# Gathers and scatters that alternate in an expert loop, and an expert's w1 copied by SyncE's DMAs

## The reference

```python
x = x + tanh(g_xattn) * xattn(layernorm(x), ctx)            # q, k from ctx (128 features), softmax, mix
h = layernorm(x)
wgt, idx = top_k(softmax(gelu(h @ rw1) @ rw2), 2)           # 8 experts, 2 for each token
for e in range(8):
    Ye = gelu(h @ w1[e] + b1[e]) @ w2[e] + b2[e]            # w1[e] 256 x 1024, w2[e] 1024 x 256
    Ce = gelu(b1[e]) @ w2[e] + b2[e]
    for k in range(2):
        mask = idx[..., k] == e
        out += any(mask) * wgt[..., k] * where(mask, Ye, Ce)
return x + tanh(g_ffn) * out
```

## Time and profile before

| what | value |
|---|---|
| time, median of 3 runs | 244.16 us (242.99, 244.16, 244.80) |
| span of the profiled execution, first to last instruction | 240.2 us |
| PE, matmul busy | 174.1 us, 72% |
| VectorE busy | 178.3 us, 74% |
| ACT busy | 96.2 us, 40% |
| GpSimd busy | 118.0 us, 49% |
| expert loop, from the first half of pair 2 to that of pair 9 | 124.64 to 213.26 us |
| mean granted TensorE clock | 0.876 |

### The profile page before, as it was taken

How to read it: one execution, slowest core, us unless ns; L and a number is a source line. 1 busy time by engine, 2 the same in 40 slices (tenths; PEclk the granted TensorE clock), 3 DMA queues, 4 the chain that set the end, 5 groups by cost and what they waited for, 6 DMA issues and landing times.

```text
span 240.2 us, 5593 instructions
## 1 busy us (share of the span) xinstructions
PE 174.1 (72%) x1708; PEld 141.8 (59%) x1709; DVE 178.3 (74%) x352; ACT 96.2 (40%) x230; POOL 118.0 (49%) x144
## 2 busy tenths in 40 slices
PE   7876638818500176729997989989797979799691
PEld 2455426317400133629887979889797979687370
DVE  1399998999999899596956776767675767656264
ACT  1369527656585700603333342423333334233000
POOL 0033365991789209992337282746455464632100
PEclk9997988976855557779999999999999999999955
DMA  7893564785887504101001111110102020100096
GB/s 190 280 381 118 175 213 145 249 282 193 271 302 256 189 3 130 45 1 46 20 21 46 44 44 32 32 55 15 57 22 66 20 66 22 46 15 27 31 289 233
DMA packets 20625, 28.05 MB, mean 117 GB/s; under 512 B 2341, under 2 KB 17407, under 8 KB 20610
## 3 DMA queue, kind: packets, MB, share of 16 engines
q1 hardware_dynamic: 16768, 21.94, 27.6%
q0 software_dynamic: 1872, 4.73, 6.3%
q10 hardware_dynamic: 1970, 1.19, 1.8%
HBM read 23.64 MB, written 4.60 MB: 118 GB/s over the span
## 4 chain that ended last, share of the span: by engine, by line
DVE 36%; PE 30%; DMA 14%; issue 10%; POOL 3%; ACT 2%; POOLq 2%; SPq 1%; DVEq 0%; ACTq 0%
DMA probT<-x_table,gcol 8%; PE bank L1065 4%; DVE lnx L562 4%; PE bank L1066 4%; PE bank L1067 4%; PE bank L1075 4%; PE bank L1077 4%; PE bank L1076 4%; DVE w_lo L539 4%; DMA xs<-in_x 4%; DVE cf L765 2%; POOL gcol L326 2%; DMA stage<-y_table 2%; DVE prob L588 2%; ACT w_hi L399 2%
## 5 line engine op out<-in xcount | busy, mean ns | idle before, releaser
L512 ACT ACTIVATE lnx<-bank,b1T 128x128 f32<-128x128 f32 x152 | 43.3, 367 | 78.6 <-PE bank L1067 72.2
L316 POOL TENSOR_TENSOR w_lo<-stage,w_hi 128x1024 bf16<-128x1024 f32 x23 | 50.3, 2212 | 35.2 <-ACT w_hi L399 35.1
L1065 PE MATMUL bank<-cfT,stage 128*128 128x128 f16 x272 | 52.6, 219 | 0.0
L1066 PE MATMUL bank<-cfT,stage 128*128 128x128 bf16 x272 | 52.6, 219 | 0.0
L1067 PE MATMUL bank<-cfT,stage 128*128 128x128 f16 x272 | 52.6, 219 | 0.0
L1075 PE MATMUL bank<-w_hi,cf 128*128 (+1 forms) x152 | 41.8, 275 | 5.6 <-DVE lnT L767 5.5
L1077 PE MATMUL bank<-w_hi,lnT 128*128 (+1 forms) x152 | 41.7, 275 | 0.0
L1076 PE MATMUL bank<-w_lo,cf 128*128 (+1 forms) x152 | 41.7, 274 | 0.0
L399 ACT ACTIVATE w_hi<-stage 128x1024 f16<-128x1024 f32 x32 | 32.4, 1051 | 20.1 <-DMA stage<-in_L_ffn_w 17.5
L322 POOL TENSOR_TENSOR held<-cst 128x1 f32<-128x1 f32 x39 | 12.1, 310 | 47.1 <-DVE qT L774 44.8
L1065 PEld LDWEIGHTS bank<-cfT,stage 128*128 128x128 f16 x272 | 26.6, 98 | 1.5
(11 more groups left out here) (168 smaller groups left out, 321.6 us busy)
## 6 DMA issues: line engine op xcount, KB each, us to landing
stage<-in_L_ffn_w SPq DMA_DIRECT2D x32, 512.0 KB, 4.1
stage<-y_table SPq DMA_DIRECT2D x8, 256.0 KB, 4.2
xs<-in_x SPq DMA_DIRECT2D x1, 1024.0 KB, 8.4
out<-stage SPq DMA_DIRECT2D x4, 256.0 KB, 3.5
cf<-in_ctx SPq DMA_DIRECT2D x1, 512.0 KB, 4.7
x_table<-cfT ACTq DMA_DIRECT2D x2, 256.0 KB, 2.6
x_table<-probT ACTq DMA_DIRECT2D x2, 256.0 KB, 4.2
probT<-x_table,gcol POOLq DMA_INDIRECT x20, 2.8
```

The source lines that it names most:

```text
L316: nc.gpsimd.tensor_tensor(out=w_lo[:, q, :], in0=stage[:, q % RING, :], in1=w_hi[:, q, :], op=ALU.subtract).then_inc(lo_pool, 1)
L512: last = nc.scalar.activation(hidden[u][:, cc * P:cc * P + P], bank[(0 if u == 0 else 6) + half][:, c * P:c * P + P], ACT.Gelu, bias=b1T[: ...
L1065: mm(o, wh, xh[:, d, :], start=(d == 0), stop=False)
L1066: mm(o, wh, xl[:, d, :], start=False, stop=False)
```

## The change

There are two edits. In GpSimd's program the order within iteration j becomes gather(j+1, 0), scatter(j-1, 0), gather(j+1, 1), scatter(j-1, 1). The scatter of an even block is therefore issued one iteration later in the program than before, and the pieces ahead of and behind the loop are adapted. And `fetch_w1` goes from VectorE to SyncE: the two copies become two DMAs from SBUF to SBUF, of 128 x 4 KB each, issued after the same wait on `h_done`. Each slot u has a semaphore of its own, and SyncE has a loop over the pairs.

```diff
+            def fetch_w1(j, u):
+                e = sp.value_load(eb[0:1, bass.ds(2 * j + u, 1)], min_val=0, max_val=N_EXP - 1)
+                if not isinstance(j, int) or j > 1:
+                    sp.wait_ge(h_done, 4 * j + 2 * u - 2)
+                for h in range(2):
+                    sp.dma_start(w1f[:, u, h, :].bitcast(I32).unsqueeze(1),
+                                 w1_words[h][:, bass.ds(e, 1), 0:QW]).then_inc(w1_fetched[u], 16)
+
+            sp.wait_ge(index_ready, 2)
+            wait_weights(sp, QUARTERS - 5)
+            fetch_w1(1, 0)
+            wait_weights(sp, QUARTERS - 3)
+            fetch_w1(1, 1)
+            wait_weights(sp, QUARTERS - 1)
             sp.wait_ge(used_ready, 1)
             jl, odd = last_pair(sp), odd_blocks(sp)
+            with sp.Fori(2, JN - 1) as j:
+                with sp.If(j < jl):
+                    for u in range(2):
+                        fetch_w1(j, u)
+            for u in range(2):
+                fetch_w1(jl, u)
             sp.wait_ge(scattered[0], 16 * jl + 16)
...
-            def pair(j, first=False, last=False):
...
-                elif not second(j) and not last:
-                    for u in range(2):
-                        wait(tr_x, 2 * j + u + 1)
-                        wait(gathered[u], 16 * j)
-                        gather(j + 1, u)
...
-                        wait(scattered[1], 16 * (j - 1))
-                    scatter(j - 1, 1)
-                    wait(scattered[0], 16 * j)
-                scatter(j, 0)
...
+            def refill(j, u):
+                wait(tr_x, 2 * j + u + 1)
+                wait(gathered[u], 16 * j)
+                gather(j + 1, u)
+
+            def put(j, u):
+                if not isinstance(j, int) or j:
+                    wait(scattered[u], 16 * j)
+                scatter(j, u)
+
+            def pair(j):
+                refill(j, 0)
+                put(j - 1, 0)
+                refill(j, 1)
+                put(j - 1, 1)
...
             with pool.Fori(2, JN - 1) as j:
                 with pool.If(j < jl):
                     pair(j)
-            pair(jl, last=True)
+            for u in range(2):
+                put(jl - 1, u)
+            put(jl, 0)
             with pool.If(2 * jl + 1 < used):
-                wait(scattered[1], 16 * jl)
-                scatter(jl, 1)
+                put(jl, 1)
...
-            def fetch_w1(i, u):
-                e = dve.value_load(eb[0:1, bass.ds(i, 1)], min_val=0, max_val=N_EXP - 1)
-                if not isinstance(i, int) or i > 3:
-                    dve.wait_ge(h_done, 2 * i - 2)
-                for h in range(2):
-                    nc.vector.tensor_copy(w1f[:, u, h, :].bitcast(I32).unsqueeze(1),
-                                          w1_words[h][:, bass.ds(e, 1), 0:QW]).then_inc(w1_fetched, 1)
...
                 if c == 0:
                     pe.wait_ge(xT_ready, i + 1)
                     if e is None:
-                        pe.wait_ge(w1_fetched, 2 * i - 2)
+                        pe.wait_ge(w1_fetched[u], 16 * (i - u))
```

More of the change, by code:

```diff
@@ L211, in flamingo_moe_kernel @@
         dlg_ready, elg_ready = sem("dlg_ready"), sem("elg_ready")
-        w1_fetched = sem("w1_fetched")
+        w1_fetched = [sem("w1_fetched0"), sem("w1_fetched1")]
         gcol_ready, ycol_ready = sem("gcol_ready"), sem("ycol_ready")
@@ L352, in _ @@
             lows(LATE, QUARTERS)
-            def pair(j, first=False, last=False):
-                if first:
-                    for u in range(2):
-                        wait(tr_x, u + 1)
-                        wait(gathered[u], 16)
-                        gather(2, u)
-                elif not second(j) and not last:
-                    for u in range(2):
-                        wait(tr_x, 2 * j + u + 1)
-                        wait(gathered[u], 16 * j)
-                        gather(j + 1, u)
[L365 to L368, removed]
-                        wait(scattered[1], 16 * (j - 1))
-                    scatter(j - 1, 1)
-                    wait(scattered[0], 16 * j)
-                scatter(j, 0)
-            pair(0, first=True)
-            pair(1)
+            def refill(j, u):
[12 more added lines that the diff above has]
+            for u in range(2):
+                wait(tr_x, u + 1)
+                wait(gathered[u], 16)
+                gather(2, u)
+            wait(index_ready, 2)
+            for u in range(2):
+                put(0, u)
             pool.wait_ge(used_ready, 1)
@@ L815, in _ @@
             hidden_split(0, 0, 1)
-            wait_weights(dve, QUARTERS - 5)
-            fetch_w1(2, 0)
             hidden_split(0, 1, 0)
@@ L835, in pair @@
                 hidden_split(j - 1, 1, 1)
-                fetch_w1(2 * j + 1, 1)
                 hidden_split(j, 0, 0)
@@ L840, in pair @@
                 hidden_split(j, 0, 1)
-                fetch_w1(2 * j + 2, 0)
                 hidden_split(j, 1, 0)
                 y_copy(j, 0)
-            wait_weights(dve, QUARTERS - 3)
             pair(1)
-            wait_weights(dve, QUARTERS - 1)
             dve.wait_ge(used_ready, 1)
@@ L854, in _ @@
             hidden_split(jl - 1, 1, 1)
-            fetch_w1(2 * jl + 1, 1)
             hidden_split(jl, 0, 0)
```

## The result

The change makes the kernel faster: 233.6 us (median of 4 runs, 232.97 to 235.18) against 243.57 of the kernel before (4 runs), a ratio of 0.960 with a 95% interval of 0.955 to 0.966. The forecast was 234.5. In a later job the same kernel stood at 0.964 (0.960 to 0.967).

The account below looks back on a forecast made before the run. The prediction took PE's seven waits for gathers stuck behind scatters as the loop's removable loss: -10.5 us plus 0.8 for late fetches gives -9.7, so 244.16 becomes 234.5 us. Range 233.3 to 243, the forecast's own 233.4 to 237.

Parts of the forecast that it names:

- The stall and its place: Expert loop: PE's first transpose waits seven times for a gather queued behind a scatter; removing this gains 10.65 us, 10.5 used.
- 0.8 us for late fetches: Expert loop: allowance of 0.1 us a pair over 8 pairs for w1 fetches that come late by chance.
- What would be late next: Expert loop after the alternation: nothing else late; both gathers have 4.3 us slack, GpSimd needs 4.4 of 5.53 us a half.
- rival 3: Expert loop: no gain, the order moves the wait and GpSimd becomes the bound; 244 us, chance 2%.
- off the path: gain 0: VectorE's four w1 copies a pair, 0.69 us each: not on the critical path, so removing them gains 0.
- F = 5.0 to 5.8: SyncE's w1 fetch per block: time F from wake-up through landing to PE resuming, 5.0 us, 5.8 with gathers and scatters.
- threshold of 5.92 us: Expert loop: time available to a w1 fetch between a block's last up matmul and the next use of its slot.
- A gather beside a fetch: Shared DMA engines: a gather is delayed up to 2.93 us by queue, 1.46 by turn-taking; slack 4.3 us holds the former.
- The 3.96 us above the span: Whole kernel: the three runs' median stands 3.96 us above the profiled span, carried over to the forecast time.
- The ends: Before and behind the loop: first fetches covered, last scatter and loads as before; cost 0.
- Slower by half a rate from SBUF to SBUF: Rival 1, expert loop: the fetch sets the period, F 7.9 or 8.7 us; 249 or 255 us, chance 15%.
- Part of the gain: Rival 2, expert loop: F between 5.92 and 7.4 us gives back 3 to 9 us; 237 to 243 us, chance 15%.

## Why the prediction was right, point by point

- **The stall and its place.** Right: L1035, the gather behind the scatter, seven times. I had -10.65 us for the loop; it was -10.15, and -10.6 in the kernel with the alternation alone (88.62 to 78.00). All of it comes from this edit. That the whole sum came so near, -9.7 us against -8.7 and -10.0 in the medians of two jobs, is in part luck: I had taken off 0.8 us for late fetches, of which there were none, and 0.5 us were lost in the loop by something else, the next point.
- **What would be late next.** I said nothing, from slacks of 4.3 us. No wait for a gather was left; GpSimd needed 42.3 us of 78.47, so that rival 3 was far off. What I did not see is VectorE's entry into its own loop: VectorE was idle for 2.21 us between the y_copy ahead of it and its copy to xT, in place of 1.42 with its old program, and PE waited 0.4 us. I know of no row of before that would have shown it.
- **VectorE's copies, "off the path: gain 0".** Right for the sum and wrong as a reading of the profile. In the old order they were on the path: the 0.73 and 0.53 us that I took as the price of the gather's copy and hold were 0.20 and 0.19 us of work and the rest a wait for VectorE's copies of the earlier trace rows, which run at that very time (177.79 to 179.09). Two of the kernels show it, one by taking the copies away (239.21 us) and one by putting copies back that nobody reads (243.45). The two edits don't add: in the job that had all three kernels they bring 9.1 and 3.9 us alone and 8.7 together, since both shorten one chain, and the alternation takes it off the path. The Trainium skill, "SBUF — State Buffer" (who interferes with whom), says that such a VectorE copy and GpSimd share a pair of ports and that the second to come is held up for the whole instruction; by that each of the two held instructions should end just behind a VectorE copy. The trace agrees, at 0.03 and 0.06 us.
- **The fetch, F = 5.0 to 5.8.** On the safe side. In the run with the first fetch held back, where the trace has the landings, a DMA of a fetch lands after 3.6 us at the median, and the second is issued 0.6 us behind the first: 4.2 us, and 0.35 for the two wake-ups make an F of about 4.5. So the 0.8 us that I allowed for fetches that come late were not needed. The Trainium skill's price for SBUF to SBUF ("SBUF — State Buffer", its summary of rules), by which I had an estimated F of 4.5, was the better one, and 397 GB/s at a share of 0.97 is within a tenth of its 436. My threshold of 5.92 us holds in kind: with 0.5 MB more w1 comes just in time and once too late, 1.05 MB more makes w1 the limit. Above it my sum was too kind, since it left out the gathers and scatters.
- **A gather beside a fetch.** By the queue I had up to 2.93 us more, by the Trainium skill's turn-taking of queues ("DMA: Bandwidth & Descriptors", queues, rings and completion order) up to 1.46. It was 0.6 more, 3.40 to 2.82, in the one place where PE waited for it. That fits both bounds and doesn't tell them apart. The 1.46 also rested on a misreading: by the earlier trace rows, 1296 packets for 3.23 MB, a packet of a gather or scatter is 2.5 KB in the mean, not a row of 1 KB, so a gather has some 53 packets and an engine 3 or 4 of them, not 8. By turn-taking these would be held up by an estimated 0.55 to 0.7 us, near the 0.6 that was seen.
- **The 3.96 us above the span.** Carried over rightly, and read wrongly: it is not what lies before the first and after the last instruction. In most listed runs the time is 1.8 to 2.0 us above that run's own span (233.93 against 232.1 in the profile after). The rest is the distance of the profiled execution from its kernel's median.
- **The ends.** I set them at 0. The changed kernel's first fetches did come in idle time (103.18 us and later) and cost nothing that shows; behind the loop 0.25 us were lost.
- **The rivals.** Slower by half a rate from SBUF to SBUF: excluded by 397 GB/s. Part of the gain, and no gain: excluded by halves of 5.53 us.

## What to carry to other kernels

An instruction that waits in an in-order queue delays everything behind it, so let work that is ready early (a gather with a free slot) alternate with work that waits, and read the gain as the distance between the actual and the undisturbed period. Durations of tiny GpSimd instructions are not prices: where one form takes 0.19 us here and 0.53 there, look at what VectorE does at that moment before you call VectorE's work free. And when two edits shorten the same chain, try each alone: here the simpler one had the whole gain, and the other was worth nothing beside it.

## What the runs showed of the hardware that was not expected

- A cast of VectorE that takes 0.42 us took 6.25 us while GpSimd ran three subtractions of 128 x 1024 in a row (6.27 us for the three), and 6.59 us in another execution: it did not get in between them. With the three on VectorE at about 1.2 us each it took 0.42 us again.
- 1.05 MB from SBUF to SBUF in two DMAs of 4 KB rows: 397 GB/s while PE was busy all the time at the upper clock, and PE's halves stayed at 5.53 us.
- Pauses in PE's work that were 1.4 us longer, just ahead of the loop, were followed by a granted clock of 0.72, in place of 1.00, over the six microseconds from 104 us, which cost an estimated 1.7 us more, 24 matmuls.
